# Attention scores of four heads in two row tiles of 64 partitions, with block-diagonal keys of half the width

## The reference

```python
qh = (q @ Wq.T + bq).reshape(B, QN, H, DH).transpose(0, 2, 1, 3)
kh = (k @ Wk.T + bk).reshape(B, KN, H, DH).transpose(0, 2, 1, 3)
...
qh = layernorm(qh, q_gamma, q_beta) * scale
kh = layernorm(kh, k_gamma, k_beta)
attn = jax.nn.softmax(jnp.einsum('bhqd,bhkd->bhqk', qh, kh), axis=-1)
x = jnp.einsum('bhqk,bhkd->bhqd', attn, vh)
x = x.transpose(0, 2, 1, 3).reshape(B, QN, E)
return x @ Wp.T + bp
```

## Time and profile before

| | |
|---|---|
| runs | 1766.55, 1766.66, 1753.21 us; median 1766.55 |
| profiled execution | span 1760.9 us from the first to the last instruction, granted TensorE clock 0.910 on the mean |
| TensorE matmul busy | 1525.1 us, 87% of the span |
| TensorE weight loads busy | 1177.3 us, 67% |
| VectorE / GpSimd / ScalarE busy | 834.1 / 705.8 / 540.4 us |
| first attention | first score matmul at 151.8 us, last at 435.5 us |

### The profile page before, as it was taken

One profiled execution on the slowest core, in us unless ns is written; L12 is line 12 of the kernel. 1 busy time (PEld: TensorE's weight loads), 2 busy tenths in 40 slices (PEclk: granted clock), 3 DMA queues, 4 the chain that ended last, 5 costly groups with the idle time before them and its releaser, 6 DMA issues. The chain is left out here.

```text
span 1760.9 us, 31109 instructions
## 1 busy us (share of the span) xinstructions
PE 1525.1 (87%) x7835; PEld 1177.3 (67%) x7837; DVE 834.1 (47%) x2214; ACT 540.4 (31%) x1136; POOL 705.8 (40%) x1120
## 2 busy tenths in 40 slices
PE   7996999999687999999995899868689999978940
PEld 3565999999534888888884777634478888744520
DVE  3573666666673232323232566579723333335443
ACT  1243444444423222222221344322033333310100
POOL 0111423332523222222214677223266666637675
PEclk9797999999656999999996899979899999999975
DMA  2116111111102111111114856311165554745443
GB/s 78 36 36 250 48 46 45 45 36 47 45 24 72 54 48 53 48 53 49 51 38 159 271 167 175 104 60 36 42 205 159 160 156 149 142 126 153 140 127 100
DMA packets 115216, 168.80 MB, mean 96 GB/s; under 512 B 17107, under 2 KB 95573, under 8 KB 112854
## 3 DMA queue, kind: packets, MB, share of 16 engines
q1 hardware_dynamic: 90630, 100.20, 16.8%
q0 software_dynamic: 20352, 55.60, 12.4%
q10 hardware_dynamic: 4176, 12.27, 2.1%
HBM read 110.87 MB, written 57.15 MB: 95 GB/s over the span
## 5 line engine op out<-in xcount | busy, mean ns | idle before, releaser
L1824 POOL DMA_INDIRECT m_xg<-t_xn,m_idx x160 | 153.0, 956 | 91.0 <-issue 82.8
L1930 PE MATMUL psum<-gu,m_xT 128*128 x640 | 152.5, 381 | 0.0
L1992 POOL DMA_INDIRECT su_yg<-t_y,su_idx x128 | 125.5, 981 | 56.9 <-issue 35.8
L1230 PE MATMUL psum<-w,m_hT 128*128 x576 | 136.3, 380 | 0.8 <-ACT m_hT L1149 0.8
L1168 DVE TENSOR_TENSOR m_h<-psum,m_h 128x512 f32<-128x512 f32 x72 | 49.8, 692 | 165.1 <-ACT m_h L1143 165.1
L1930 PEld LDWEIGHTS psum<-gu,m_xT 128*128 128x128 f32 x640 | 116.3, 192 | 12.8
L695 PEld LDWEIGHTS psum<-kv,at_prT 77*128 77x128 f32 x1024 | 121.8, 195 | 0.0
L695 PE MATMUL psum<-kv,at_prT 77*128 (+1 forms) x1024 | 121.2, 260 | 0.0
L1209 PE MATMUL psum<-w,m_xT_high 128*128 x288 | 120.8, 419 | 0.0
L1889 DVE TENSOR_TENSOR m_h<-psum,m_sg 128x256 f32<-128x256 f32 x80 | 34.0, 425 | 181.8 <-ACT m_sg L1868 112.3
L1209 PE MATMUL psum<-w,m_xT_low 128*128 x288 | 114.2, 397 | 0.0
(11 more groups left out here) (264 smaller groups left out, 3352.0 us busy)
## 6 DMA issues: line engine op xcount, KB each, us to landing
t_y<-m_y SPq DMA_DIRECT2D x80, 256.0 KB
t_x<-at_x SPq DMA_DIRECT2D x96, 128.0 KB, 2.2
w<-in_w SPq DMA_DIRECT2D x8, 1024.0 KB
gu<-in_gu ACTq DMA_DIRECT2D x8, 1024.0 KB
t_y<-top_v SPq DMA_DIRECT2D x36, 128.0 KB
t_y<-top_i SPq DMA_DIRECT2D x36, 128.0 KB
w<-in_x SPq DMA_DIRECT2D x16, 256.0 KB, 2.7
at_x_in<-in_x SPq DMA_DIRECT2D x32, 128.0 KB
```

The costliest lines, as they stand in the source:

```text
L1230: last = pe.matmul(ps_y[:, 0:D], hT[:, c * P:(c + 1) * P], g.w2[:, bass.ds(ex * (MC * D) + c * D, D)], start=(c == 0), stop=(c == MC - 1))
L1824: pool.indirect_dma_start(out=xg[p][:, k * D:(k + 1) * D], out_offset=None, in_=g.xn4, in_offset=bass.IndirectOffsetOnAxis(ap=idx[p][k][:, ...
L1930: last = pe.matmul(ps_gu[p][:, k * 2 * M1:(k + 1) * 2 * M1], xT[p][:, at:at + P], g.gu[:, bass.ds(ex[k] * (DC * 2 * M1) + c * 2 * M1, 2 * ...
L1992: pool.indirect_dma_start(out=yg[p][k][:, :], out_offset=None, in_=g.y1, in_offset=bass.IndirectOffsetOnAxis(ap=idx[p][:, k:k + 1], axis=0))\
```

## The change

The score matmuls take 64 partitions each. The first (a = 0) multiplies partitions 0 to 63 of the queries, which hold heads 0 to 3 of the group, with partitions 0 to 63 of kblk; the second (a = 1) partitions 64 to 127, heads 4 to 7. kblk has for each group 308 columns in place of 616: in column block j stand the keys of head j in the upper half of the partitions and those of head 4 + j in the lower half. The mask has 4 columns, the same pattern twice.

```diff
-        hmask = sb("hmask", [P, HG])
+        hmask = sb("hmask", [P, HG // 2])
         q_s = [sb(f"q_s{i}", [P, D]) for i in range(2)]
-        kblk = [sb(f"kblk{i}", [P, NG * HG * LK]) for i in range(2)]
+        kblk = [sb(f"kblk{i}", [P, NG * HW]) for i in range(2)]
...
                             pool.tensor_tensor(
-                                kblk[bp_][:, gr * HG * LK:(gr + 1) * HG * LK].rearrange("p (h k) -> p h k", h=HG),
-                                kT.unsqueeze(1).broadcast_to([P, HG, LK]),
-                                hmask[:, :].unsqueeze(2).broadcast_to([P, HG, LK]), ALU.mult).then_inc(k_ready, 1)
+                                kblk[bp_][:, gr * HW:(gr + 1) * HW].rearrange("p (h k) -> p h k", h=HG // 2),
+                                kT.unsqueeze(1).broadcast_to([P, HG // 2, LK]),
+                                hmask[:, :].unsqueeze(2).broadcast_to([P, HG // 2, LK]), ALU.mult).then_inc(k_ready, 1)
...
                     for a in range(2):
-                        last = pe.matmul(ps_s[:, a, 0:HW], q_s[p][:, gr * P:(gr + 1) * P],
-                                         kblk[b.mod(2)][:, (2 * gr + a) * HW:(2 * gr + a + 1) * HW],
-                                         start=True, stop=True)
+                        own = slice(a * P // 2, (a + 1) * P // 2)
+                        last = pe.matmul(ps_s[:, a, 0:HW], q_s[p][own, gr * P:(gr + 1) * P],
+                                         kblk[b.mod(2)][own, gr * HW:(gr + 1) * HW], start=True, stop=True)
                     last.then_inc(s_mm, 1)
...
-        "hmask": np.repeat(np.eye(HG, dtype=f), DH, axis=0),
+        "hmask": np.tile(np.repeat(np.eye(HG // 2, dtype=f), DH, axis=0), (2, 1)),
```

## The result

The changed kernel takes 1814.9 us (median of 5 runs, 1810.42 to 1842.28) against 1766.15 us of the kernel before. The ratio is 1.0294, with a 95% interval of 1.0253 to 1.0335: slower by some 49 us, where I had forecast no difference. Each experiment's ratio is to runs of the kernel before on the same chip, whose medians were 1762.32 to 1765.76 us.

What follows compares the result with a forecast made beforehand. TensorE's unbroken train of matmuls was taken to bound the first attention. Shape changes +18.7, overlap -16.5 and shorter start -0.85 summed to +1.3 us on 1766.55, about 1768 us, range 1749 to 1788.

Steps and rivals of the forecast that it cites:

- What bounds the stage: First attention: TensorE's unbroken train of matmuls sets the time, busy 279.89 of 280.00 us; other engines wait for it.
- The switch: Scores on TensorE: entering and leaving the 64-row shape empties the array, 0.585 us a pair of units, +18.7 us.
- What overlaps: Score matmuls side by side: queue order lets one of four slots be hidden, 0.517 us a pair, -16.5 us.
- rival of full overlap: Both score matmuls side by side throughout, two slots hidden: -15.2 us in all, 1751 us, period near 8.65; chance 0.08.
- The start: GpSimd's two first builds of kblk, which the first scores wait for, get shorter: 0.85 us for both.
- Worse: Moving between row halves also empties the array, up to +31 us, 1797 us, or the granted clock falls; chance 0.08.
- signs of being wrong: Profile after: an unforeseen period, TensorE waiting for another engine in the stage, or clock under 1.00 between 200 and 400 us.

Runs made afterwards that it cites:

- e6: The changed kernel with each unit's two score matmuls computed twice, in the order A, A, B, B (A rows 0 to 63, B rows 64 to 127); 1806.34 us, one execution.
- e9: e2 with one matmul of 64 rows and 8 columns added ahead of each unit's scores, its result overwritten; 1854.82 us, ratio 1.0479.
- e2: The kernel before, full rows, with each score matmul computing only 154 of its 308 columns after the first unit; 1728.44 us, ratio 0.9821.
- e1: The changed kernel with the value matmuls widened from 17 to 102 columns by reading the value columns six times over; 1750.44 us, ratio 0.9934.
- e8: The changed kernel with the value columns read three times over, 51 columns per value matmul; 1753.21 us, ratio 0.9927.
- e3: The changed kernel with both score matmuls reading rows 0 to 63, so nothing runs side by side; 2028.8 us, ratio 1.1493.
- e5: The changed kernel with each unit's two score matmuls computed twice, in the order A, B, A, B (A rows 0 to 63, B rows 64 to 127); 1799.05 us, ratio 1.0186.
- e4: The changed kernel with four of each unit's eight transposes done twice; 1790.68 us, ratio 1.0171.
- e7: The kernel before with the value matmuls widened from 17 to 102 columns; 1764.02 us, ratio 0.9989.
- e10: The changed kernel with both score matmuls in rows 0 to 63 and the value matmuls widened to 102 columns; 1824.59 us, one execution.

## Why the prediction was wrong

*What bounds the stage* was right. TensorE's train is what lasts, before and after, and no other engine became late.

*The switch* was sized well. Entering after L731, from its end to the scores' end, is now 216.17 - 215.45 = 0.72 us, two slots of 0.517 and 0.20 (I had 0.19). Leaving is 217.20 - 216.17 = 1.03 us for eight transposes that took 0.88: 0.15, as forecast from the one-row tiles. The whole is 8.67 - (9.10 - 1.034) = 0.61 us a pair against 0.585. By the Trainium skill ("TensorEngine Tiling (Array Packing)", Key Properties) a change of tiling mode drains TensorE; the trace agrees, with these 0.15 to 0.20 us.

*What overlaps* was wrong. I took "a matmul starts only once the one ahead of it in the queue has started" from rows of the trace in which every matmul shared rows of the array with the one before it; they could not show otherwise. e6 shows that it doesn't hold between row tiles. Two slots are hidden, not one: -33.1 us and not -16.5. This was my rival of full overlap, with 0.08, and at full clock it came out at its 8.65 (8.67). By that step alone the forecast would have been too high. The Trainium skill has both sides: its independent tiles ("TensorEngine Tiling (Array Packing)", Key Properties) agree with the runs, its strict FIFO of matmul starts and ends ("TensorE: Matmul & The Clock Gate", Part 3) doesn't hold for different row tiles in e6.

*The start* was right: two builds take 1.36 us in place of 2.39, 1.03 less where I had 0.85.

*The step that failed* is the clock. I had it under "Worse": "the granted clock falls from 1.00 while half the rows rest; the qkv stage with its one-row matmuls keeps 1.00 in 80 to 120 us, which speaks against it", and gave it no price. The term was 79 us: 65.1 in the stage and the 13.8 that the tiling won. A clock under 1.00 between 200 and 400 us stood among my signs of being wrong, and that is the sign that came. The reason against it was weak in two ways. A stage that keeps its clock says nothing of another's margin. And the fall has another cause than resting rows: no row rests in the changed kernel while scores flow, since the two tiles fill the array. What brings it down is that the scores flow half as long and the array changes its shape twice a unit, the two together (e9). The short scores alone don't do it (e2); whether the changes of shape alone would was not run. I summed what the train gains and loses in time and never asked what it does to the share of the time in which columns flow, although a switch and an overlap both lower it: in the kernel before, two units have four score slots each and no gap, now two and 0.6 us of emptying. That this share is what counts is my inference from the runs; none of them varies it alone. Giving flow back in a place that costs no time restores the clock (e1, e8), and at full clock the tiling's gain shows: 0.9934 and 0.9927 against a control of 0.9989, all three within 1% of the kernel before.

What stays open is how much a transpose, a 64-row tile and two of them side by side each count towards the clock. e3 against e5 shows that one tile at a time counts less than two, and e4 and e5 that added transposes and side-by-side tiles help but gave 0.94 and 0.95, where e2's shorter train had 1.00.

## What to carry to other kernels

When a change makes matmuls shorter on an engine that never waits, ask what it does to the granted clock, not only to the sum of slots: a busy share of 100% says nothing of it (40.00 of 40.00 us at a clock of 0.62, from 320 to 360 us), for here the profile counted as busy both the matmuls that take as long as their weight loads and the time that a change of shape costs. Where TensorE has matmuls bound by their weight loads, wider ones are free (102 columns in place of 17 cost 0.02 us in 9.10, e7) and can hold the clock. Row tiles pay at full clock even when the shape changes twice in 4.3 us, but what they gain is only what lies above 0.15 to 0.2 us a change (8.69 against 9.12 us for two units, e1 and e7).

## What was unexpected of the hardware

Matmuls of different row tiles overtake each other: with four passes for rows 0 to 63 standing ahead, the first pass for rows 64 to 127 began within 0.02 us of the first of those (e6). The clock was 0.51 over the whole stage in e3, though TensorE was busy for 160.00 of the 160 us from 240 to 400, and fell to 0.62 to 0.80 in the changed kernel, where a change of shape costs 0.15 to 0.2 us and nothing else interrupts the train. The Trainium skill's advice on keeping the clock up speaks of idle gaps between bursts of matmuls ("TensorE: Matmul & The Clock Gate", section "Why this matters for your kernels"); no such gap was here, and the clock fell all the same. From the lower level it can also come back late: e10, in its one execution, ran at 0.54 from 200 to 240 us and then at 1.00 with the same instructions.
